# Row maxima of an attention block contracted over one 32-row block, two units at a time, on one Trainium2 core

## The reference, cut to what matters

```python
scores = jnp.einsum('bhqd,bhkd->bhqk', q, k) / jnp.sqrt(jnp.float32(hd))
scores = jnp.where(causal, scores, jnp.finfo(scores.dtype).min)
attn = jax.nn.softmax(scores, axis=-1)
```

## Time and profile before

| | us |
|---|---|
| median of three executions | 1057.57 |
| the profiled execution, own time | 1060.96 |
| its span, first to last instruction | 1059.2 |
| busy in the span: PE | 907.8 |
| DVE | 827.8 |
| ACT | 729.2 |
| POOL | 590.5 |

### The profile page before, as it was taken

One profiled execution on the slowest core, in us unless ns is written; L12 is line 12 of the kernel. 1 busy time (PEld: TensorE's weight loads), 2 busy tenths in 40 slices (PEclk: granted clock), 3 DMA queues, 4 the chain that ended last, 5 costly groups with the idle time before them and its releaser, 6 DMA issues. The chain is left out here.

```text
span 1059.2 us, 26980 instructions
## 1 busy us (share of the span) xinstructions
PE 907.8 (86%) x7519; PEld 724.8 (68%) x7519; DVE 827.8 (78%) x2292; ACT 729.2 (69%) x1795; POOL 590.5 (56%) x781
## 2 busy tenths in 40 slices
PE   2469999999999999999999988840999999999474
PEld 1347777776776777766777666520999999999421
DVE  2459899899899999988989777665677777766378
ACT  4766898888888878878876554530766776666356
POOL 8001344446666666767677666874466666665400
PEclk9568999999999999999999989965999999999788
DMA  1045454435445445435443544052333333332196
GB/s 55 13 107 136 108 124 117 112 89 134 120 120 130 104 116 137 130 94 134 119 115 103 148 113 132 23 131 80 98 98 98 94 87 97 97 90 63 39 254 191
DMA packets 138080, 115.22 MB, mean 109 GB/s; under 512 B 18400, under 2 KB 126564, under 8 KB 137968
## 3 DMA queue, kind: packets, MB, share of 16 engines
q1 hardware_dynamic: 120880, 92.76, 34.5%
q0 software_dynamic: 8640, 16.93, 5.0%
q10 hardware_dynamic: 8448, 4.20, 1.4%
HBM read 61.12 MB, written 52.58 MB: 107 GB/s over the span
## 5 line engine op out<-in xcount | busy, mean ns | idle before, releaser
L577 POOL TENSOR_SCALAR_AFFINE_SELECT b_PT<-b_PT 128x256 f32<-128x256 f32 (+1 forms) x384 | 193.6, 518 | 202.2 <-ACT b_PT L763 198.3
L1074 DVE TENSOR_REDUCE b_m_neg<-b_ps_m 128x2 f32<-128x512 f32 (+1 forms) x384 | 256.1, 680 | 56.8 <-PE b_ps_m L1476 35.2
L763 ACT ACTIVATE b_PT<-b_ps_s 128x512 f32<-128x512 f32 x384 | 223.7, 599 | 63.6 <-PE b_ps_s L1455 35.3
L1798 POOL DMA_INDIRECT results<-e_Y,e_X x142 | 161.8, 1139 | 106.4 <-issue 68.3
L1826 ACT ACTIVATE e_h<-e_ps,e_w 128x256 f32<-128x256 f32 x284 | 111.8, 475 | 77.1 <-PE e_ps L1899 71.3
L612 POOL DMA_INDIRECT slots<-c_pay,b_pos x128 | 128.7, 1006 | 43.2 <-issue 31.1
L1906 PE MATMUL e_ps_y<-e_w,e_h 128*128 128x128 f32 x1136 | 140.4, 277 | 3.0 <-ACT e_h L1826 3.0
L1906 PEld LDWEIGHTS e_ps_y<-e_w,e_h 128*128 128x128 f32 x1136 | 134.4, 194 | 3.3 <-ACT e_h L1826 3.3
L1476 PE MATMUL b_ps_m<-c_QK 128*128 128x256 f32 x512 | 121.0, 325 | 0.0
L1455 PE MATMUL b_ps_s<-c_QK 128*128 128x512 f32 x256 | 118.3, 471 | 2.5 <-ACT b_PT L763 2.1
L1469 PE MATMUL b_ps_m<-c_QK 128*128 128x128 f32 x512 | 96.7, 312 | 0.0
(11 more groups left out here) (217 smaller groups left out, 2188.1 us busy)
## 6 DMA issues: line engine op xcount, KB each, us to landing
c_QK<-qk_scr SPq DMA_DIRECT2D x128, 192.0 KB
qk_scr<-b_qk_hi SPq DMA_DIRECT2D x64, 256.0 KB
e_X<-slots SPq DMA_DIRECT2D x71, 130.0 KB
qk_scr<-b_qk_lo SPq DMA_DIRECT2D x32, 256.0 KB
f_G<-results SPq DMA_DIRECT2D x32, 256.0 KB, 3.6
a_X<-in_L_attn_x_dram SPq DMA_DIRECT2D x16, 256.0 KB
x<-a_X SPq DMA_DIRECT2D x16, 256.0 KB
b_X<-x SPq DMA_DIRECT2D x32, 128.0 KB
```

Of the source, the lines that this page charges most:

```text
L577: nc.gpsimd.affine_select(out=tri, in_=tri, compare_op=ALU.is_ge, fill=0.0, base=0, pattern=[[0, tri.shape[1]], [1, P]], channel_multiplie ...
L763: nc.scalar.activation(PT[:, g % 2, q % 3], ps_s[:, q % 2], ACT.Exp, scale=HD ** -0.5).then_inc(s_e, 1)
L1074: nc.vector.tensor_reduce(out, scores, AX.X, ALU.max, negate=True).then_inc(s_red, 1)
L1798: nc.gpsimd.indirect_dma_start(dram["results"][:, :], bass.IndirectOffsetOnAxis(X[:, j.of(NB_X), u, D:D + 1].bitcast(u32), 0), Y[:, n, u, ...
```

## The change

- Each maxima product contracts only the 24 rows of its own block (`QK[at, ...]` with rows 32j to 32j+23) in place of 128 rows.
- Units are handled in pairs. `maxima(b, pair)` makes units 2 pair and 2 pair + 1: first both mask products, then the products of the two units alternately. The two units of a pair are on different blocks j and in different banks. It waits until both units of the pair before have been reduced.
- The unit numbers mean something else (`unit`): units 0 to 3 now take one block j with its four groups, units 4 to 11 one block with two groups.
- Row 24 is no longer read by the maxima, so `zero_row`, its memset and the zeroing transfer are gone, and a turn is ready after four transfers in place of five.
- The calls in `step` are in another order on PE, DVE and ACT; on POOL one mask moves ahead of one send.

```diff
-        WRITES, READS = 3 * 16, 5 * 16
-        FILLED = 3 + 2 * NQ
+        WRITES, READS = 3 * 16, 4 * 16
+        FILLED = 2 + 2 * NQ
+        def unit(u):
+            if u < 4:
+                return u, 0
+            return 2 * ((u - 4) // 4) + u % 2, 2 * ((u - 4) // 2 % 2)
...
-                    sync.dma_start(QK[M_ROW:M_ROW + 1, n, 0:NJ].rearrange("o j g n -> o (j g) n").bitcast(fp32), zero_row[:, :]).then_inc(s_qkr[n], 16)
...
-            def maximum(b, u):
+            def maxima(b, pair):
...
-                need(pe, s_red, 12 * b + (u - 1))
...
-                    for j in range(4):
-                        done = nc.tensor.matmul(ps_m[:, u % 2, j * P:(j + 1) * P], QK[:, n, j, u, 0:P], QK[:, n, NJ, u, 0:P],
-                                                start=False, stop=(j == 3), skip_group_check=True)
...
+                need(pe, s_red, 12 * b + 2 * pair)
+                for u in units:
+                    if u < 4:
+                        nc.tensor.matmul(ps_m[:, u % 2].rearrange("p (g k) -> p g k", g=NG), ident_b[:, :], mask_b[:, :, :],
+                                         start=True, stop=False, skip_group_check=True)
...
+                last = NG if pair < 2 else 2
+                for i in range(last):
+                    for u in units:
+                        j, g = unit(u)
+                        at = slice(32 * j, 32 * j + ROWS)
+                        if u < 4:
+                            done = nc.tensor.matmul(ps_m[:, u % 2, i * P:(i + 1) * P], QK[at, n, j, i, 0:P], QK[at, n, NJ, i, 0:P],
+                                                    start=False, stop=(i == last - 1), skip_group_check=True)
+                        else:
+                            done = nc.tensor.matmul(ps_m[:, u % 2, i * T:(i + 1) * T], QK[at, n, j, g + i, P:T], QK[at, n, NJ, g + i, :],
+                                                    start=False, stop=(i == last - 1), skip_group_check=True)
+                        if i == last - 1:
+                            done.then_inc(s_b, 1)
```

More of the change, by code:

```diff
@@ L494, in step @@
                 if (s - 1).exists(B):
+                    b, n = s - 1, (s - 1).of(NQ)
+                    need(sync, s_qkw[n], b.turn(NQ) * WRITES + WRITES)
                     need(sync, s_s, (b - NQ) * 12 + 12)
@@ L529, in _ @@
         def _(pool):
-            nc.gpsimd.memset(zero_row[:, :], 0.0).then_inc(s_fill, 1)
             nc.gpsimd.memset(V[:, :, :, :], 0.0).then_inc(s_fill, 1)
-            pool.wait_ge(s_fill, 2)
+            pool.wait_ge(s_fill, 1)
             for n in range(NV):
@@ L631, in step @@
                     cell_divisor(gi)
+                    mask(c, 1)
                     sends(s, 1)
-                    mask(c, 1)
                     mask(c, 2)
@@ L662, in weights @@
                 nc.scalar.copy(by_place(w_p), by_set(w_f)).then_inc(s_whi, 1)
-                act.wait_ge(s_fill, 3)
+                act.wait_ge(s_fill, 2)
                 act.wait_ge(s_prep, 1)
@@ L1456, in score @@
                                      start=True, stop=True).then_inc(s_s, 1)
-            def maximum(b, u):
+            def maxima(b, pair):
                 if not b.exists(B):
                     return
-                n = b.of(NQ)
-                if u == 0:
+                n, units = b.of(NQ), (2 * pair, 2 * pair + 1)
+                if pair == 0:
                     need(pe, s_qkr[n], b.turn(NQ) * READS + READS)
-                need(pe, s_red, 12 * b + (u - 1))
-                if u < 4:
-                    nc.tensor.matmul(ps_m[:, u % 2].rearrange("p (j k) -> p j k", j=4), ident_b[:, :], mask_b[:, :, :],
-                                     start=True, stop=False, skip_group_check=True)
-                    for j in range(4):
-                        done = nc.tensor.matmul(ps_m[:, u % 2, j * P:(j + 1) * P], QK[:, n, j, u, 0:P], QK[:, n, NJ, u, 0:P],
-                                                start=False, stop=(j == 3), skip_group_check=True)
-                else:
-                    g, jp = divmod(u - 4, 2)
-                    nc.tensor.matmul(ps_m[:, u % 2].rearrange("p (j k) -> p j k", j=2)[:, :, P:T], ident_b[:, :], mask_b[:, 0:2, :],
-                                     start=True, stop=False, skip_group_check=True)
-                    for j in range(2):
-                        done = nc.tensor.matmul(ps_m[:, u % 2, j * T:(j + 1) * T], QK[:, n, 2 * jp + j, g, P:T], QK[:, n, NJ, g, :],
-                                                start=False, stop=(j == 1), skip_group_check=True)
-                done.then_inc(s_b, 1)
@@ new lines, in maxima @@
+                need(pe, s_red, 12 * b + 2 * pair)
[4 more added lines that the diff above has]
+                    else:
+                        nc.tensor.matmul(ps_m[:, u % 2].rearrange("p (g k) -> p g k", g=2)[:, :, P:T], ident_b[:, :], mask_b[:, 0:2, :],
+                                         start=True, stop=False, skip_group_check=True)
```

189 lines of the change are left out of this document (87 added, 102 removed).

## The result

The changed kernel took 1119.81 us (median of 4, 1112.72 to 1128.48), the kernel before 1058.67 in the same comparison: ratio 1.0582, 95% interval 1.0482 to 1.0682. The forecast was 1069.6 in a range of 1036 to 1098. Slower was right; the size, +61 where +12 was forecast, was not.

The account below looks back on a forecast made before the run. PE was taken to bound periods without routing, DVE routed ones. Only the 24-row products counted, +12 us, with pairs, transfer and order at 0: 1057.6 + 12 = 1069.6 us, range 1036 to 1098.

Parts of the forecast that it names:

- What bounds it: Layers phase, 100 to 600 us: PE bounds periods without routing, DVE routed ones; about 8 of 16 periods each.
- Part 1: 24-row maxima products on PE: shape-change gaps outweigh overlap, +0.76 us per sequence, +1.5 per period, 12 us in all.
- the 8 periods bound by PE: Steady-part periods without routing, where 1.5 us more PE time each was to count in full, 12 us.
- the 37.4 of the forecast: Sign of being right: periods without routing at about 37.4 us, from 35.9 before.
- the clock as a condition: PE's clock should stay at 1.00 from 100 to 600 us; if it falls, none of the sums holds.
- Part 2: Waiting for both units of the pair before: in PE-bound periods replaces waits DVE already has (2.4 us); counted as nothing.
- The second rival: DVE waits for pairs: 1.5 us in all 16 periods, 24 us, giving 1082; chance 0.15.
- Part 3: 32 one-row zeroing transfers leave SP's queue: between 0 and -1 us, taken as 0.
- Part 4: New call order: little to find on PE, up to 18 us on DVE, as much to lose; taken as 0.
- PE's slack of 2.8 us: PE's wait for a bank's reduce in routed periods, to cover the 24 rows' 1.5 us; routed periods stay near 41.
- The first: Shape change of rows costs little or nothing: 22 us faster, capped by DVE's idle time, 1036; chance 0.28.
- The third: 24-row products on PE do not overlap: 58 us slower, 1116; chance 0.07.

Follow-up runs that it names:

- the experiment: The changed kernel with the zeroing transfer put back ahead of the loads into QK, all else as changed: 1109.58 us, ratio 1.0476 to the kernel before.

## Why the prediction was wrong, by its own steps

- **What bounds it.** At most half right. PE waits only 0.3 us in the period without routing, as read, but that does not make it the bound: 3.8 us taken off PE (no masks) shorten this period by 0.3 us and an early one by 2.0. A next limit stands close behind; that it is the round from a bank's reduce to PE and back is argued from the price of the pairs below and not shown here.
- **Part 1, 24 rows.** The price (0.88 for a pair; 0.86 measured) and the overlap of two products were right. The step that failed is the sum: 12 us "in the 8 periods bound by PE". Early periods did become 37.6 us (17.9 + 19.7), near the 37.4 of the forecast, but by luck: with 128 rows in the same pairs they take 37.5, and the later period that the 37.4 was worked out for takes 39.0 (19.2 + 19.8), and 39.2 with 128 rows. So the gaps as such are worth next to nothing here; what the rows cost is the clock, 18.7 us from the first reduce to the last. That 12 is of the size of 18.7 is luck, too. The prediction named the clock as a condition and gave its failure no price and no chance.
- **Part 2, pairs.** "I count nothing in the sum" is the term that failed most: 16.5 us, half for the wait, half for the longer way of both banks through PE. "Such waits replace waits that DVE has already" is what the rows refute: from the new order alone to pairs over 128 rows, from 100 to 600 us, PE's waits for reduces rise from 15.6 to 31.9 us and DVE's ahead of reduces from 25.0 to 44.8. The second rival had the mechanism, at 24 us, and was given 0.15; it should have been a term.
- **Part 3, no zeroing transfer.** Forecast 0; the experiment cannot tell it from 0, within a few us.
- **Part 4, the order.** "I take 0" between bounds of 18 either way: 8.4 us lost in the profiled run, 14 by the medians (10 to 18). The routed periods did find 0.8 us each, and the others lost twice that. Ahead of the loss in the step's middle stands a late pair of reduces whose releaser the profile of the changed kernel calls "remote"; why it is late stays open. What the trace shows: in all seven such waits of the changed kernel the pair's products had ended 1.6 us or more before, and the reduce starts 0.7 to 0.9 us behind a run of three of POOL's L614 transfers (288.47 and 289.27 in the step from 275.3). No run tests whether the two belong together.
- **The routed periods.** PE's slack of 2.8 us was to cover Part 1. The four between 233.2 and 523.9 take 42.1 to 43.8 us for the 41 forecast, and the two rows above (20.8 + 22.3 = 43.1) hold a fall of the clock in the first.
- **The rivals.** The first fell: gaps of rows are as large as those of columns. The Trainium skill (TensorEngine Tiling (Array Packing), Key Properties) has a change of mode drain TensorE; the 0.32 us from mask to first product, for 0.15 with 128 rows, agrees with it. The third fell with the 0.43 us for four products.

So four terms add up where the forecast had one: order 8.4, wait 8.3, way 8.2, clock 18.7, in all 43.6 of the 51.8 us of span between the two profiled executions; 3.6 lie ahead of the first reduce and 4.6 behind the last.

## What to carry to other kernels

Where two engines hand a pair of banks to and fro, what counts is the round trip: whatever makes one side wait for both banks, or fills both together, takes away the overlap for which there were two, even if each engine has time to spare; here either cost 8 us. Price such a wait as a term, not as a rival, and try the order, the wait and the shape of a change one by one before paying for them together. And a forecast for a kernel that keeps PE at its full clock needs a price for losing it: take it from rows at either level.

## What the runs showed that was not expected

The same products, in the same order, left the granted clock at 0.99 over 128 rows, 0.97 over 64 and 0.95 over 24, between the first and the last reduce; with 64 and 24 rows their start-to-start times are the same as well. Over all executions and the whole span it is 0.924 to 0.936, 0.921 to 0.928 and 0.891 to 0.908 (0.887 to 0.916 with the transfer put back): 24 rows stand apart, 64 and 128 overlap. The 64-row run was made to tell rows from changes of shape, and as the shape changes as often there as with 24 rows, the changes alone do not set it. They are not excluded as a part, since going from 128 to 64 rows brings both. Nor are few rows needed: in the old order 128-row pairs had 0.95 between their first and last reduce, and the kernel before had 0.97 without its masks, for 0.99 with them. Twice the mask products in the changed kernel raised it from 0.96 to 0.98 (100 to 600 us). What the chip weighs in this is not shown.
